# Order of a pipelined AdaLN attention block: maxima rows, values, fillings, and banks of the last transposed scores

## The reference

```
mod = (silu(c) @ wmod).reshape(16, 6, 1, 256)       # sa, ca, ga, sb, cb, gb
h = layernorm(x) * (1 + ca) + sa
x = x + ga * attention(h)                           # 16 heads of 16, causal mask, softmax
h = layernorm(x) * (1 + cb) + sb
first = argmax(softmax(h @ Wg.T)) == 0              # for each token
x = x + gb * where(first, gelu_mlp(h), relu_mlp(h)) # two experts, 256 -> 512 -> 256
```

## Time and profile before

| | us |
|---|---|
| median of 3 runs (lowest, highest) | 626.19 (624.16, 627.58) |
| profiled execution, its own time | 626.41 |
| its span | 624.6 |
| busy: PE, VectorE (DVE), ScalarE (ACT), POOL | 476.7, 433.9, 291.4, 222.7 |
| mean granted TensorE clock, as a share of full speed | 0.883 |
| moved by DMA | 80.44 MB, 129 GB/s in the mean |

### The profile page before, as it was taken

The page is one execution under the profiler, slowest core; times in us unless marked ns, Lnnn a source line. Parts: engine busy times, 40 slices in busy tenths (PEclk is TensorE's granted clock), DMA queues, the critical chain, the costliest instruction groups (busy, mean ns, idle before and its releaser), DMA issues. The chain is left out here.

```text
span 624.6 us, 11638 instructions
## 1 busy us (share of the span) xinstructions
PE 476.7 (76%) x4137; PEld 379.4 (61%) x4137; DVE 433.9 (69%) x988; ACT 291.4 (47%) x425; POOL 222.7 (36%) x241
## 2 busy tenths in 40 slices
PE   4733797797887977978979779798601899999960
PEld 3432575686675765856757568575401798889850
DVE  4565474686967968869679787686532479998980
ACT  2342264354544544545445535445400666767640
POOL 8312121223334234243342431422452005554565
PEclk9857797997988979989789898899965799999995
DMA  9579548457477475674574754732475924460111
GB/s 251 172 87 118 70 96 127 65 99 154 94 147 160 102 138 124 148 154 98 130 162 104 150 122 117 148 103 96 136 193 189 375 79 135 152 213 9 35 50 50
DMA packets 58376, 80.44 MB, mean 129 GB/s; under 512 B 6975, under 2 KB 47040, under 8 KB 58320
## 3 DMA queue, kind: packets, MB, share of 16 engines
q1 hardware_dynamic: 53392, 59.76, 45.3%
q0 software_dynamic: 4928, 19.95, 9.7%
HBM read 34.12 MB, written 20.53 MB: 87 GB/s over the span
## 5 line engine op out<-in xcount | busy, mean ns | idle before, releaser
L1105 DVE TENSOR_REDUCE mx<-ps_s 128x2 f32<-128x512 f32 (+1 forms) x192 | 124.0, 685 | 88.2 <-PE ps_s L440 87.4
L856 ACT ACTIVATE p_all<-ps_t 128x1024 f32<-128x1024 f32 x96 | 98.5, 1026 | 150.8 <-PE ps_t L440 150.7
L480 PE MATMUL ps_t<-qs,ks 99*128 99x256 bf16 (+1 forms) x512 | 63.5, 263 | 54.6 <-DMA qs<-mx_rows 48.6
L460 PE MATMUL ps_s<-ks,qs 96*128 96x256 bf16 (+1 forms) x512 | 79.6, 265 | 19.4 <-issue 9.8
L480 PEld LDWEIGHTS ps_t<-qs,ks 99*128 99x128 bf16 x512 | 42.6, 105 | 66.7 <-DMA qs<-mx_rows 48.0
L440 PE MATMUL ps_s<-future_b,ident_b 128*128 128x256 bf16 (+1 forms) x192 | 63.9, 333 | 0.0
L460 PEld LDWEIGHTS ps_s<-ks,qs 96*128 96x128 bf16 x512 | 40.6, 105 | 36.4 <-issue 22.8
L1356 POOL TENSOR_TENSOR comb<-z,xs 128x512 f32<-128x512 f32 x16 | 20.3, 1270 | 94.2 <-DVE z L1168 84.0
L440 PE MATMUL ps_t<-past_b,ident_b 128*128 128x256 bf16 (+1 forms) x192 | 49.2, 340 | 0.0
L1463 POOL TENSOR_TENSOR tile_rows<-tile_rows 128x512 f32<-128x512 f32 x18 | 26.3, 1463 | 62.1 <-DVE tile_rows L1288 62.0
L1400 POOL TENSOR_TENSOR h_lo<-h,h_hi 128x512 fp32r<-128x512 f32 x16 | 23.1, 1446 | 62.1 <-ACT h_hi L782 62.1
(11 more groups left out here) (205 smaller groups left out, 1260.3 us busy)
## 6 DMA issues: line engine op xcount, KB each, us to landing
qs<-parts_q SPq DMA_DIRECT2D x96, 128.0 KB
ks<-parts_k SPq DMA_DIRECT2D x96, 128.0 KB, 4.9
tile_rows<-sorted_scratch SPq DMA_DIRECT2D x9, 1026.0 KB, 12.2
rows<-mod_rows_scratch SPq DMA_DIRECT2D x16, 384.0 KB, 3.6
tile_rows<-sorted_scratch SPq DMA_DIRECT2D x9, 512.0 KB, 4.8
xs<-x SPq DMA_DIRECT2D x16, 256.0 KB, 4.9
comb<-mod_rows_scratch SPq DMA_DIRECT2D x32, 128.0 KB, 4.4
p_all<-wmod SPq DMA_DIRECT2D x1, 1024.0 KB, 6.6
```

Of the source, the lines that this page charges most:

```text
L460: pe.matmul(ps_s[:, n * width:(n + 1) * width], qs[b.third][0:R, h, tile * P:(tile + 1) * P], ks[b.third][0:R, h, 0:width], start=n % a_ba ...
L480: pe.matmul(ps_t[:, h * width:(h + 1) * width], ks[b.third][0:RM, h0 + h, tile * P:(tile + 1) * P], qs[b.third][0:RM, h0 + h, tile * P:S], ...
L856: act.activation((p0, p1)[tile][:, h0:h0 + n, :], ps_t[:].rearrange("p (h s) -> p h s", h=n), ACT.Exp, scale=SCALE).then_inc(exp_done, 1)
L1105: dve.tensor_reduce(mx[:, tile, h0:h0 + n], ps_s[:, 512 * bank:512 * (bank + 1)].rearrange("p (h k) -> p h k", h=n), AX_X, ALU.max).then_i ...
```

## The change

Six edits in the orders and waits; no arithmetic changes. SyncE issues load_maxima(at(3)) ahead of all stacks. PE does expand_v(at(1)) ahead of st_chunk(at(3), 0), and ScalarE v_copy(at(1)) ahead of exponentials(at(3), 0). POOL does inverse_deviation(at(5), 1) ahead of put_rows(at(6)). FILL_BATCH becomes NB - 5 = 11, so the fillings are (512 + 4 * 256) / 128 = 12, at the end of POOL's step 17, and put_rows(12) waits for them. For the last batch, odd chunks of transposed scores go to ps_s, whose own scores are done by then, and each chunk waits for the exponentials of one chunk fewer.

```diff
-        FILL_BATCH = NB - 3
+        FILL_BATCH = NB - 5
...
+        def scores_t(b, c):
+
+            return ps_s if b.n == NB - 1 and c % 2 else ps_t
...
                 rest_of_weights(at(0))
+                load_maxima(at(3))
                 stack_q(at(1), 0)
-                load_maxima(at(3))
                 stack_q(at(1), 1)
...
-                wait(pe, exp_done, CH * b.n + c)
+                dst = scores_t(b, c)
+                if b.n == NB - 1:
+                    wait(pe, exp_done, CH * b.n + max(c - 1, 0))
+                    if c == 1:
+                        pe.wait_ge(max_done, 2 * CH * NB)
+                else:
+                    wait(pe, exp_done, CH * b.n + c)
...
-                    pe.matmul(ps_t[:, h * width:(h + 1) * width], ks[b.third][0:RM, h0 + h, tile * P:(tile + 1) * P],
+                    pe.matmul(dst[:, h * width:(h + 1) * width], ks[b.third][0:RM, h0 + h, tile * P:(tile + 1) * P],
...
-                    mm = masked(ps_t[:, bank * 512:(bank + 1) * 512], a_bank, 0, past_b)
+                    mm = masked(dst[:, bank * 512:(bank + 1) * 512], a_bank, 0, past_b)
...
                 values(at(4), 3)
+                expand_v(at(1), ("Q", at(1)))
                 st_chunk(at(3), 0)
-                expand_v(at(1), ("Q", at(1)))
...
-                act.activation((p0, p1)[tile][:, h0:h0 + n, :], ps_t[:].rearrange("p (h s) -> p h s", h=n), ACT.Exp, scale=SCALE).then_inc(exp_done, 1)
+                act.activation((p0, p1)[tile][:, h0:h0 + n, :], scores_t(b, c)[:].rearrange("p (h s) -> p h s", h=n), ACT.Exp, scale=SCALE).then_inc(exp_done, 1)
...
                 values_copy(at(4), 1)
+                v_copy(at(1))
                 exponentials(at(3), 0)
-                v_copy(at(1))
...
+                inverse_deviation(at(5), 1)
                 put_rows(at(6))
-                inverse_deviation(at(5), 1)
                 k_third(at(1))
```

## The result

| us | before | changed |
|---|---|---|
| median (lowest, highest) | 626.16 (624.16, 627.58) | 593.12 (590.56, 594.27) |
| profiled execution, its own time | 626.41 | 590.56 |
| its span | 624.6 | 588.8 |
| busy: PE, VectorE, ScalarE, POOL | 476.7, 433.9, 291.4, 222.7 | 467.5, 434.2, 295.1, 227.6 |
| granted clock | 0.883 | 0.907 |

The ratio is 0.9469, interval [0.9428, 0.9509]: 5.3% faster, where 565 us and a range of 551 to 588 were forecast. The direction was right; the gain is 33 us instead of 61, and the time lies 5 us above the range.

The account below looks back on a forecast made before the run. PE seemed the bound, inflated by waits for the maxima rows and half clock; its own need was 19.3 us a step, VectorE's 19.75. Gains of 55.1 (steps) + 6 (fillings) = 61 us from 626 gave 565, range 551 to 588.

Parts of the forecast that it names:

- The issue follows at once: SyncE, each step: the maxima are issued at 291.12, right after their copy ends at 291.10, instead of at 293.43.
- loses nothing: PE, each step: after expand_v it reaches the transposed scores at 295.2 without waiting, or loses 0.5 us at the other bound.
- VectorE's 4.04 us: VectorE's idle time in a step, from the end of second_stats at 297.46 to 301.50, forecast to go.
- term (b): Each step's last k stack, possibly late next: lands at 305.3, 306.2 or 307.8; PE wants it at 306.4.
- rival B: The last k stack becomes the bound, behind puts and saturated DMA: period 22.1 to 23.5, 573 to 596 us; chance 0.18.
- its own ring: The cycle through the last k stack in each step, which gave a period of 19.6 to 22.1 us.
- three chains that meet: Chains in a step ending within 0.4 us of each other, 20.3 to 20.7; the period was taken as 21.2.
- Step 3: An early step without puts and with a wait of over 4 us: 4.4 us to be gained.
- The first three go out some 0.5 us later: SyncE, each step: the first three q stacks, now behind the wait for the maxima's copy, start at 291.96 instead of 291.53.
- nothing waits for q before the k stacks are in: Each step: the claim beside the first three q stacks' 0.5 us delay; no separate size given.
- Fillings in step 17: Tail: twelve fillings hold POOL 15.0 us in step 17 instead of eight in step 19; gain 6 us (2 to 9).
- the some 5 us lost in step 18: Tail: add_attn(13) comes 8 us late behind POOL's fillings, costing VectorE and PE about 5 us.

Follow-up runs that it names:

- g1: The changed kernel with all transposed scores of the last batch in ps_t again, with the old waits: 591.97 us.
- g2: The changed kernel with expand_v and v_copy back behind the transposed scores and exponentials, maxima still first: 594.03 us.
- e5: The changed kernel with SyncE's load_maxima behind stack_q(at(1), 0) again: 599.34 us.
- f1: The kernel before with fill_slot 12 columns wide instead of 8, so qs0 starts at a multiple of 256 bytes: 608.95 us.
- f2: The changed kernel with fillings back in step 19 and fill_slot kept 12 columns wide, so addresses stay: 586.99 us.
- e1: The changed kernel with POOL's put_rows(at(6)) ahead of inverse_deviation(at(5), 1) again: 577.22 us.
- e4: The changed kernel with FILL_BATCH = NB - 3 (eight fillings, step 19), which also puts qs0 224 bytes past a multiple of 256: 615.93 us.
- h2: The changed kernel with 32 bytes of padding ahead of qs, so qs0 starts 32 past a multiple of 256: 624.04 us.
- h3: The changed kernel with 64 bytes of padding ahead of qs, so qs0 starts 64 past a multiple of 256: 617.46 us.
- h1: The kernel before with SyncE's load_maxima first and nothing else, qs0 at its old address: 614.03 us.
- g4: f4 with 256 bytes of padding ahead of qs, so that qs0 starts at a multiple of 512: 577.77 us.
- f4: The changed kernel with e1's POOL order, fill_slot kept 12 columns wide as in f1, and fillings in step 19: 573.5 us.

## Why the prediction was right and wrong

**Right.** "The issue follows at once" and "loses nothing" at the transposed scores: 0.40 us behind the start of the copy, no wait. VectorE's 4.04 us gone, clock 1.00 all through step 13, DMA share 0.75 for 0.74, k_third behind inverse and puts, POOL held for 15 us, the wait of 5.62 in step 20 gone. Four banks, costed at 0: g1, without them, is 1.2 us faster, with intervals that overlap. The order of expand_v and v_copy, which no run takes apart, is worth nothing that g2 can tell once the maxima are early, in line with PE "loses nothing"; with late maxima it may hide part of the wait (e5 against f1, which has the old order, 9.6 us; but the other edits are in that too).

**The last k stack, term (b).** This is the step that failed in the steps of the pipeline. The walk took "3.5, 4.4 or 6.0 us after its issue" and let the median decide. Its k_third was right (forecast to end 11.1 us behind the copy, measured 298.05 + 1.18 - 289.01 = 10.2), but the scores began 305.87 - 299.23 = 6.6 us behind it. The median of the earlier trace rows was taken over twelve stacks, and in the kernel before the first three go out to idle engines (DMA share 0.00 from 291.50 to 292.50). The last one stands behind all of them. The most of the row, 6.0, would have given a period of 22.1, and 21.97 was measured. That is rival B (chance 0.18) in its mechanism, and 593 us lies in its 573 to 596. Its period, 22.1 to 23.5, begins just above the 21.97 of this profile; f2 and g1, with the same instructions and addresses in these steps, show 22.50 and 22.17, so a profile tells a period to half a us. The period was forecast as 21.2 though its own ring went to 22.1: three chains that meet should have been read by their slowest, and 0.5 us was added where 1.3 was wanted. The half clock behind the wait was in no sum; the four stretches that have it cost 4 x 1.6 us, 0.5 us a step in the mean. That POOL's new order ends k_third 1.5 us later was seen, but by the median landing it cost nothing; it is worth some 15 us (e1).

**Step 3.** Forecast 4.4 us gained, measured 3.2 lost. "The first three go out some 0.5 us later" and "nothing waits for q before the k stacks are in" were taken from step 12. That is the step that failed here. In step 3 of the kernel before the first stack was issued 0.75 us ahead of the copy (68.70, copy at 69.45); now SyncE stands at the maxima until 1.33 us behind it. Twelve stacks go out 2.1 us later, PE waits 4.65 us in step 4, and the slow clock costs 2.8 more (7.77 for 5.02). All kernels with the maxima first take 23.8 to 25.0 us here; f1 and e5, which have not, 19.8 and 20.8. A repeated step's rows don't hold for the first one.

**Fillings in step 17.** Forecast 6 us gained (2 to 9), measured 8 less than that. The sum followed POOL and the landing to batch 15, and took the some 5 us lost in step 18 as covered. That term failed: step 17 becomes 12.25 us longer, which eats the 10.1 us by which the rest of the first part is shorter. POOL's hold, from which the loss was worked out, isn't it, since POOL was free 3.50 us before add_attn(13) had its input; PE's own product ran at a quarter of its pace beside the fillings, and why stays open. The gain at the end was real.

**The address.** It was in no step. The prediction went through the edits as orders and waits and priced a constant only by what it counts, not by the memory that its tensor takes. It was worth 29 us in f2 against e4, 31 in the changed kernel against h2, and 24 against h3. With it left out the forecast of 565 would have been wrong by 52 (h3) to 59 us (h2), not 28. Off the multiple of 256 all the edits together are worth 2 us (h2) or 9 (h3). Maxima first alone gains 12 there (h1), as most of the removed wait comes back at the last k stack, and the other edits give some of it back. That the forecast came as near as 28 us is luck.

## What to carry to other kernels

When a wait is removed, price the next one by the last transfer of its queue, not by the median of all, and where several chains meet, take the slowest. When a constant changes, look at what it sizes: an unrelated tensor that grows by 16 bytes moved every DMA destination behind it. Before several edits are judged, run the one-line ones alone and at fixed addresses; here maxima first and the 32 bytes of one constant hold all of the gain, and the others together lose 15 us of it.

## What the runs showed of the hardware

DMAs from SBUF to SBUF ran at 130 GB/s where the written tensors start at a multiple of 256 bytes in their partitions, at 118 where they start 224 (e4) or 32 bytes (h2) past it, and at 120 at 64 past it (h3), with full DMA engines in each case. The kernel was no faster at a multiple of 512 (g4 577.77 us, f4 573.5). Where sources moved instead, the rate stayed at 129. In a kernel whose period hangs on these DMAs, 10% of rate became 5% of time.

Beside twelve indirect DMAs of 128 rows of 3 KB, with the DMA engines 0.85 busy, twelve matmuls without a wait between them took 6.2 us instead of 1.7.
